# Seven counter increments ahead of the two loops of layer 1's experts

## The chip, the cores and the metric

The kernel runs on one core of one Trainium2 chip. The metric is the time of one execution on the device in microseconds. Before the change the median of 3 runs is 2973.64 us (2965.7 to 2974.67).

## What is computed

Two layers in float32 over 2048 token rows of width 512. Layer 0 is a state-space block over a context, then a mixture of experts; layer 1 is cross-attention, then a mixture of 32 experts with 8 chosen per token. Only that last mixture matters here:

```python
gate = jax.lax.ragged_dot(xs, w_gate, group_sizes)
up = jax.lax.ragged_dot(xs, w_up, group_sizes)
down = jax.lax.ragged_dot(jax.nn.silu(gate) * up, w_down, group_sizes)
routed = (down[unsort].reshape(T, K, H) * tkw[..., None]).sum(axis=1)
shared = jax.nn.silu(x @ sw_gate) * (x @ sw_up) @ sw_down
return (routed + shared).reshape(hidden_states.shape)
```

Every token row is copied once per expert that it goes to, the rows are grouped by expert, each group goes through gate, up and down of its expert, and the results are added back, scaled, to the token's row. An expert's weights are 512 x 256 for gate and up and 256 x 512 for down.

## The kernel before

`program` calls one function per stage: `mamba_stage`, `route_stage`, `expert_stage0`, `attention_stage`, `route_stage` again, and `expert_stage1`, which the change touches. Within a stage each engine has its own instruction stream, written out by hand in a function (`@block.vector`, `@block.scalar` and so on); semaphores set the order between them. There is no planner.

`expert_stage1` works on 144 tiles (`NTILE1`) of 128 rows; each half of 64 rows belongs to one expert. Per tile t the engines do this:

- SyncE loads weights of the next experts into a ring of four and announces them (`refill`, `announce`).
- ScalarE (`gate`, L1982 to L1984) computes the silu of the gate half of the product, issues loads of later rows (`reload`), scales and empties the output product (`empty`, L1991), and copies an expert's gate and up weights for the tile's second half (`copied`, L2006 to L2008).
- VectorE (`a_round`) turns the next tile's rows (`turned_rows`, L2082), copies the turned hidden rows `hT` of the tile before (L2087), makes the product `h` (L2092), works out scales and addresses (`addressed`, L2111 to L2118) and copies the down weights (`copied`, L2096 to L2100).
- TensorE turns the hidden rows of tile t - 1 (L2175), multiplies tile t by gate and up (L2166: 16 matmuls), then the hidden rows of t - 1 by down (L2188: 8 matmuls, which wait for `hT`).
- GpSimd adds the two halves' results to the output rows in device memory by two indirect DMAs (L1944), each waiting for an earlier one to land.

The rounds are of 16 tiles (`OUT`), 9 of them (`TURNS`). They are partly written out and partly loops in the program itself, with a compare and a branch at the end of the body. VectorE's round 0 is written out, rounds 1 to 7 are the loop `dve.Fori(1, TURNS - 1)` (L2148), and round 8 is written out. ScalarE's rounds 0 and 1 are written out, rounds 2 to 7 are the loop `act.Fori(2, TURNS - 1)` (L2057), and round 8 is written out. GpSimd loops over rounds 1 to 7 (L1971). TensorE has a loop of 4 tiles a turn.

`c["held"]` is a semaphore that engines count up and nobody reads. `hold` (L77) waits for a semaphore against a register's value and counts `held` up in the same instruction; `pause` (L980, a line of the route stage) counts it up alone, `dve.sem_inc(c["held"], 1)`.

Of the kernel before, what the change touches and what calls it, by code (L numbers as in the profile page):

```python
# [76 lines left out]
def hold(eng, sem, value, held):  # L77

    eng.wait_ge(sem, value)
    eng.sem_inc(held, 1)  # L80


class Pools:
# [1736 lines left out]
def expert_stage1(nc, c, I, D, x, route, W, out):  # L1820
# [3 lines left out]
    with ExitStack() as ctx:  # L1824
# [69 lines left out]
        def slots_written(eng, g):  # L1894
            count = eng.value_load(route["rows_held"][0:1, g:g + 1], min_val=16, max_val=16 * NT * K1 // LANES1)
            for lane in range(LANES1):
                hold(eng, written[lane], count, c["held"])

        with nc.Block(no_gpsimd_drain=True) as block:
# [80 lines left out]
            def _(act):  # L1980
                def gate(t, q):
                    act.wait_ge(sem["gu"], 1 + t + 1)  # L1982
                    act.wait_ge(sem["h"], 1 + t)
                    act.activation(sg[:, q % 2, :], ps_g[:, q % 2, 0:F1], ACT.Silu).then_inc(sem["sg"], 1)  # L1984

                def empty(t, q, first=False):
                    act.wait_ge(sem["down"], 1 + t + 1)
                    if not first:
                        act.wait_ge(sem["added"], 1 + t - OUT + 1)
                    act.wait_ge(sem["dest"], 1 + t + 1)  # L1990
                    act.activation(yo[:, q % OUT, :], ps_o[:, q % 2, :], ACT.Copy, scale=wrow[:, q % OUT, :])\  # L1991
                       .then_inc(sem["yo"], 1)
# [11 lines left out]
                def copied(t, q):  # L2004

                    e = act.value_load(ids[0:1, bass.ds(2 * t + 1, 1)], min_val=0, max_val=E - 1)  # L2006
                    hold(act, sem["ready"], 1 + e + 1, c["held"])
                    act.activation(cgu[:, q % 2, :, :], wgu[:, bass.ds(e % RING, 1), :, :].rearrange("p o k n -> p (o k) n"),  # L2008
                                   ACT.Copy).then_inc(sem["cgu"], 1)
# [5 lines left out]
                def reload(t, q):  # L2015
                    place, r = q % RING, q // RING % 2
                    known = isinstance(t, int)
                    group = t // RING if known else None
                    if place == RING - 2 and not (known and group + 2 >= GROUPS):
                        hold(act, sem["xsT"], 1 + t + 2, c["held"])  # L2020
                        if known:
                            rows_written(group + 2)
                        load_rows((t + RING + 2) * P, r, (0, 1))
                    if place == RING - 1 and not (known and group + 2 >= GROUPS):
                        load_rows((t + RING + 1) * P, r, (2,))
                    if place == 0 and not (known and group + 1 >= GROUPS):
                        load_rows((t + RING) * P, 1 - r, (3,))
                    if place == 1 and not (known and group + 1 >= GROUPS):
                        hold(act, sem["dest"], 1 + t - 1, c["held"])
                        load_rec((t + RING - 1) * P, 1 - r)  # L2030
# [21 lines left out]
                for q in range(1, OUT):  # L2052
                    gate(OUT + q, q)
                    reload(OUT + q, q)
                    empty(OUT + q - 1, q - 1)
                    copied(OUT + q + 2, q)
                with act.Fori(2, TURNS - 1) as i:  # L2057
                    for q in range(OUT):
                        gate(i * OUT + q, q)
                        reload(i * OUT + q, q)  # L2060
                        empty(i * OUT + q - 1, q + OUT - 1)
                        copied(i * OUT + q + 2, q)
# [10 lines left out]
            def _(dve):  # L2073
                def turned_rows(t, q, n, first=False):
                    if first:
                        dve.wait_ge(first_in, 16 * NQ)
                    elif q % RING == 0:
                        dve.wait_ge(rows_in[q // RING % 2], 16 * NQ * n)
                    if not first:
                        dve.wait_ge(sem["gu"], 1 + t - 1)  # L2080
                    part = slice(q % RING * NQ, (q % RING + 1) * NQ)
                    dve.transpose(xsT[:, q % 2, :, :].rearrange("p k (s j) -> p k s j", j=DQ),  # L2082
                                  xs[:, q // RING % 2, part, :].rearrange("p s (i k) -> p k s i", k=KH)).then_inc(sem["xsT"], 1)

                def turned_hidden(t, q):
                    dve.wait_ge(sem["htr"], 1 + t + 1)
                    dve.tensor_copy(hT[:, q % 2, :, :], ps_h[:, q % 2, 0:NW * P].rearrange("p (c s) -> p c s", s=P))\  # L2087
                       .then_inc(sem["hT"], 1)

                def product(t, q):  # L2090
                    dve.wait_ge(sem["sg"], 1 + t + 1)
                    dve.tensor_tensor(h[:, q % 2, :], ps_g[:, q % 2, F1:], sg[:, q % 2, :], ALU.mult).then_inc(sem["h"], 1)  # L2092

                def copied(t, q):

                    e = dve.value_load(ids[0:1, bass.ds(2 * t + 1, 1)], min_val=0, max_val=E - 1)  # L2096
                    hold(dve, sem["ready"], 1 + e + 1, c["held"])
                    if not (isinstance(t, int) and t < 2):
                        dve.wait_ge(sem["down"], 1 + t - 1)
                    dve.tensor_copy(cd[:, q % 2, :, :], wd[:, bass.ds(e % RING, 1), :, :].rearrange("p o k n -> p (o k) n"))\  # L2100
                       .then_inc(sem["cd"], 1)

                def addressed(t, q, n):
                    row = rec[:, q // RING % 2, q % RING, :]
                    word = token[:, q // RING % 2, q % RING * 2:q % RING * 2 + 2, 0]
                    if q % RING == 0:
                        dve.wait_ge(rec_in[q // RING % 2], 32 * n)
                    if not (isinstance(t, int) and t < OUT):
                        dve.wait_ge(sem["yo"], 1 + t - OUT + 1)
                        dve.wait_ge(sem["added"], 1 + t - OUT + 1)  # L2110
                    dve.scalar_tensor_tensor(out=mine[:, q % 2, :], in0=row[:, K1:2 * K1], scalar=slot1[:, bass.ds(t, 1)],  # L2111
                                             in1=row[:, 0:K1], op0=ALU.is_equal, op1=ALU.mult).then_inc(sem["named"], 1)
                    dve.scalar_tensor_tensor(out=pad[:, q % 2, :], in0=word, scalar=0.0,
                                             in1=spare1[0:HALF, q % 2 * 2:q % 2 * 2 + 2], op0=ALU.is_equal, op1=ALU.mult)\
                       .then_inc(sem["named"], 1)
                    dve.wait_ge(sem["named"], 1 + 2 * (t + 1))
                    dve.tensor_reduce(wrow[:, q, :], mine[:, q % 2, :], AX_X, ALU.add).then_inc(sem["chosen"], 1)
                    dve.scalar_tensor_tensor(out=dest[:, q, :], in0=pad[:, q % 2, :], scalar=-1.0, in1=word,  # L2118
                                             op0=ALU.add, op1=ALU.add).then_inc(sem["dest"], 1)

                def a_round(i, first=False, last=False):
                    for q in range(REST if last else OUT):
                        t = i * OUT + q
                        if first and q == 0:
                            dve.wait_ge(rows_in[0], 16 * NQ)
                        if not (last and q == REST - 1):
                            turned_rows(t + 1, q + 1, i * PER + (q + 1) // (2 * RING) + 1)
                        if not (first and q == 0):
                            turned_hidden(t - 1, q + OUT - 1)
                        product(t, q)  # L2130
                        addressed(t, q, i * PER + q // (2 * RING) + 1)
                        if not (last and q == REST - 1):
                            copied(t + 1, q + 1)
# [11 lines left out]
                turned_rows(0, 0, 1, first=True)  # L2145
                copied(0, 0)
                a_round(0, first=True)
                with dve.Fori(1, TURNS - 1) as i:  # L2148
                    a_round(i)
                a_round(TURNS - 1, last=True)  # L2150
# [1147 lines left out]
```

## Time and profile before

| | |
|---|---|
| median of 3 runs | 2973.64 us (2965.7 to 2974.67) |
| the profiled execution | 2954.43 us |
| its span | 2952.7 us |
| TensorE busy | 2631.0 us, 89% |
| VectorE busy | 1539.8 us, 52% |
| GpSimd busy | 1294.0 us, 44% |
| ScalarE busy | 1032.9 us, 35% |
| mean granted clock of TensorE | 0.962 |
| layer 1's experts | from about 2090 us to the end |

The profile is of one execution; all times below are from the start of its span. Busy is time in which an engine computes; register, branch and semaphore instructions and the issuing of DMAs are not counted. In a view of waits or a timeline, "[1.21 <-issue]" is idle time ahead of an instruction, with what ended it; "issue" means that it waited for nothing that the profile shows. The clock is in parts of full speed (1.00 is 2.4 GHz, 0.50 is 1.2 GHz); the mean of a stretch lies between.

### The profile page before, as it was taken

The page shows a single profiled execution, that of the slowest core. Times are in us where ns is not written, and L with a number is a line of the kernel's source. Part 1 is how long each engine was busy: PE and PEld are TensorE (multiplying, and loading weights), DVE is VectorE, ACT ScalarE, POOL GpSimd, SP SyncE. Part 2 cuts the span into 40 slices and gives each one's busy share as a digit, 9 for nine tenths or more (in the row PEclk, how much of TensorE's full clock was granted, in tenths as well). Part 3 has the DMA queues.
Part 4 walks back from the last instruction along what each step waited for, and adds up shares of the span by engine and source line. Part 5 has one row for each costly group of instructions (what it writes and reads, how often), then busy time and mean ns, then how long its engine had stood idle before and what let it go on. Part 6 is the DMA issues. An engine that isn't in the chain of part 4 may idle for free. (4 is left out here: it accounts for less than half of the span.)

```text
span 2952.7 us, 40958 instructions
## 1 busy us (share of the span) xinstructions
PE 2631.0 (89%) x11317; PEld 1089.2 (37%) x11318; DVE 1539.8 (52%) x2668; ACT 1032.9 (35%) x1305; POOL 1294.0 (44%) x935
## 2 busy tenths in 40 slices
PE   5889876699999987768999999799889999999998
PEld 2343432244444433323333333344333333333333
DVE  7999999741100033136666665551444544454554
ACT  4647464120000001023343433200344544455554
POOL 2767656312400023114564653145556656445454
PEclk8999999999999999889999999899999999999999
DMA  3333223301210269974047300154978877687764
GB/s 128 116 98 108 85 61 75 128 37 36 88 33 14 81 220 352 338 206 122 1 134 197 86 1 1 50 193 176 262 187 167 165 137 145 132 192 159 159 120 67
DMA packets 362080, 373.36 MB, mean 126 GB/s; under 512 B 85938, under 2 KB 268531, under 8 KB 361906
## 3 DMA queue, kind: packets, MB, share of 16 engines
q1 hardware_dynamic: 204098, 239.95, 26.1%
q0 software_dynamic: 45584, 93.26, 15.2%
q10 hardware_dynamic: 112224, 38.25, 6.3%
q8 instruction: 58, 0.95, 0.1%
q14 instruction: 116, 0.95, 0.1%
HBM read 231.96 MB, written 152.14 MB: 130 GB/s over the span
## 5 line engine op out<-in xcount | busy, mean ns | idle before, releaser
L1944 POOL DMA_INDIRECT out_x<-e_yo,e_dest x288 | 416.1, 1445 | 352.1 <-DMA out_x<-e_yo,e_dest 252.0
L2166 PE MATMUL e_psg<-e_wgu,e_xsT 128*64 x1152 | 522.0, 596 | 9.3 <-DVE e_xsT L2082 9.3
L2166 PE MATMUL e_psg<-e_cgu,e_xsT 128*64 128x512 f32 x1152 | 522.0, 596 | 0.0
L301 POOL TENSOR_TENSOR hc<-hs,bcst 128x1024 f32<-128x1024 f32 x128 | 300.6, 2349 | 178.9 <-DVE ps_b L521 171.7
L646 PE MATMUL ps_y<-hc,ident 128*128 128x512 f32 x512 | 240.9, 608 | 88.4 <-POOL hc L301 88.1
L2188 PE MATMUL e_pso<-e_wd,e_hT 128*64 x576 | 279.4, 608 | 33.0 <-DVE e_hT L2087 33.0
L527 DVE TENSOR_TENSOR_SCAN hs<-dA,ps_b 128x1024 f32<-128x1024 f32 x128 | 292.6, 2286 | 8.1 <-ACT dA L431 3.9
L2008 ACT ACTIVATE e_cgu<-e_wgu 128x2048 f32 x144 | 275.3, 1912 | 61.3 <-issue 33.9
L2188 PE MATMUL e_pso<-e_cd,e_hT 128*64 128x512 f32 x576 | 279.4, 608 | 0.0
L2166 PEld LDWEIGHTS e_psg<-e_wgu,e_xsT 128*64 128x64 f32 x1152 | 155.3, 138 | 259.0 <-issue 259.0
L949 ACT ACTIVATE r_sg<-r_ps_g 128x512 f32<-128x512 f32 x60 | 35.8, 597 | 525.0 <-PE r_ps_g L1258 525.0
L1277 PE MATMUL r_ps_t<-r_wd,r_h 128*128 128x512 f32 x480 | 210.9, 600 | 9.4 <-DVE r_h L1016 5.1
L1016 DVE TENSOR_TENSOR r_h<-r_ps_u,r_sg 128x512 f32<-128x512 f32 x60 | 41.4, 691 | 317.0 <-PE r_ps_u L1258 305.7
L431 ACT ACTIVATE dA<-dt,a_neg 128x511 f32<-128x511 f32 x256 | 165.3, 713 | 103.3 <-DVE hs L527 98.2
L717 POOL DMA_INDIRECT slots_in<-r_xn,scat x128 | 127.9, 999 | 165.8 <-DMA slots_in<-r_xn,scat 98.6
L2777 DVE TENSOR_REDUCE a_nm<-a_ps 128x2 f32<-128x992 f32 x128 | 146.1, 1185 | 88.4 <-PE a_ps L3021 88.0
L2539 ACT ACTIVATE a_pt<-a_ps 128x1024 f32<-128x1024 f32 (+1 forms) x128 | 126.2, 1022 | 181.4 <-PE a_ps L3038 120.6
L2092 DVE TENSOR_TENSOR e_h<-e_psg,e_sg 128x256 f32<-128x256 f32 x144 | 61.1, 425 | 233.7 <-ACT e_sg L1984 233.6
L2082 DVE STREAM_TRANSPOSE e_xsT<-e_xs 128x512 f32<-128x512 f32 x144 | 171.1, 1188 | 19.7 <-issue 8.6
L1991 ACT ACTIVATE e_yo<-e_pso,e_wrow 128x512 f32<-128x512 f32 x144 | 99.1, 688 | 234.4 <-PE e_pso L2188 215.9
L646 PEld LDWEIGHTS ps_y<-hc,ident 128*128 128x128 f32 x512 | 92.7, 191 | 231.2 <-POOL hc L301 137.0
L2100 DVE COPY e_cd<-e_wd 128x1024 f32 x144 | 101.3, 703 | 142.1 <-PE e_pso L2188 136.7
(432 smaller groups left out, 4205.7 us busy)
## 6 DMA issues: line engine op xcount, KB each, us to landing
slots_in<-zeros SPq DMA_DIRECT2D x144, 256.0 KB
e_xs<-slots_in ACTq DMA_DIRECT2D x140, 256.0 KB
bcst<-bc_rows SPq DMA_DIRECT2D x128, 256.0 KB, 4.2
e_wgu<-in_wg SPq DMA_DIRECT2D x32, 512.0 KB, 5.2
e_wgu<-in_wu SPq DMA_DIRECT2D x32, 512.0 KB, 6.5
e_wd<-in_wd SPq DMA_DIRECT2D x32, 512.0 KB, 8.3
e_w<-in_wg SPq DMA_DIRECT2D x11, 1408.0 KB, 15.9
e_w<-in_wu SPq DMA_DIRECT2D x11, 1408.0 KB, 17.6
```

Source lines behind the costliest of these rows:

```text
L301: pool.tensor_tensor(hc[:, it % 2, half(h), :], hs[:, it % 2, half(h), :], bc(bcst[:, q, 1, :], 1, HB), ALU.mult).then_inc(sem["hc"], 1)
L431: i = act.activation(dA[:, it % 2, t, 1:], dt[:, b % 2, t, 1:], ACT.Exp, scale=a_neg[:, n, t:t + 1])
L527: dve.tensor_tensor_scan(hs[:, it % 2, half(h), :].rearrange(flat), dA[:, it % 2, half(h), :].rearrange(flat), ps_b[:, :, :].rearrange(fla ...
L646: i = pe.matmul(ps_y[:, t, :], c["ident"][:, :], hc[:, it % 2, t, :], start=False, stop=False, skip_group_check=True)
L717: pool.indirect_dma_start(D["xs1"][:, :], bass.IndirectOffsetOnAxis(route["scat"][:, t, k:k + 1], 0), route["xn"][:, t, 0:H + 2 * K1 + 1], ...
L1277: i = pe.matmul(ps_t[:, j % 2, :], h[:, f, j * P:(j + 1) * P], wd[:, f, :], start=f == 0, stop=f == FC - 1)
L1944: pool.indirect_dma_start(out[:, :], bass.IndirectOffsetOnAxis(dest[:, q, s:s + 1], 0), yo[half(s), q, :], None, bounds_check=T + 2 * P - ...
L2008: act.activation(cgu[:, q % 2, :, :], wgu[:, bass.ds(e % RING, 1), :, :].rearrange("p o k n -> p (o k) n"), ACT.Copy).then_inc(sem["cgu"], 1)
L2082: dve.transpose(xsT[:, q % 2, :, :].rearrange("p k (s j) -> p k s j", j=DQ), xs[:, q // RING % 2, part, :].rearrange("p s (i k) -> p k s i ...
L2166: j = pe.matmul(ps_g[half(s), q % 2, :], xsT[:, q % 2, k, half(s)], w, start=k == 0, stop=k == KH - 1, tile_position=(0, s * HALF), skip_g ...
L2188: j = pe.matmul(ps_o[half(s), q % 2, :], hT[:, q % 2, a, half(s)], w, start=a == 0, stop=a == NW - 1, tile_position=(0, s * HALF), skip_gr ...
L2777: dve.tensor_reduce(nm[:, i % 8, 2 * z:2 * z + 2], ps[:, at:at + 2, 0:S2], AX_X, ALU.max, negate=True)\
```

## The change

A helper that counts the semaphore up n times, called once by ScalarE with 4 and once by VectorE with 3, each just ahead of that engine's loop. Nothing else is changed, and nothing reads the counter. The instructions behind the two places stand four and three instructions later in their engines' programs.

```diff
+def placed(eng, n, held):
+
+    for _ in range(n):
+        eng.sem_inc(held, 1)
...
                     empty(OUT + q - 1, q - 1)
                     copied(OUT + q + 2, q)
+                placed(act, 4, c["held"])
                 with act.Fori(2, TURNS - 1) as i:
                     for q in range(OUT):
                         gate(i * OUT + q, q)
...
                 copied(0, 0)
                 a_round(0, first=True)
+                placed(dve, 3, c["held"])
                 with dve.Fori(1, TURNS - 1) as i:
                     a_round(i)
```

## Rows read from the trace of the kernel before

**Rows 1.** The page, busy us, share of the span and instructions.

```profile
PE 2631.0 (89%) x11317; PEld 1089.2 (37%) x11318; DVE 1539.8 (52%) x2668; ACT 1032.9 (35%) x1305; POOL 1294.0 (44%) x935
```

**Rows 2.** Windows: busy us of PE, PEld, DVE, ACT, POOL; clock, DMA share, GB/s.

```profile
2095.00:2183.00 88.00, 88.00 (x506) 34.02 (x504) 46.53 (x124) 46.90 (x47) 41.97 (x41) 1.00 0.94 273
...
2376.00:2393.00 17.00, 13.80 (x62) 4.95 (x60) 5.96 (x16) 5.45 (x6) 10.27 (x7) 0.80 0.58 86
...
2762.00:2773.00 11.00, 8.40 (x54) 3.44 (x52) 5.33 (x15) 3.58 (x5) 4.78 (x4) 1.00 0.43 65
...
2855.00:2938.00 83.00, 83.00 (x480) 33.10 (x478) 43.47 (x119) 42.57 (x44) 42.07 (x30) 1.00 0.52 78
```

**Rows 3.** Waits of TensorE from 2210 us on: total us, times, longest.

```profile
PE e_pso L2188 <- DVE e_hT L2087: 23.4, 7, 7.0
```

**Rows 4.** Timeline of VectorE, two tiles: start, us, line, operation, idle before.

```profile
2397.20 0.42 DVE L2092 TENSOR_TENSOR e_h<-e_psg,e_sg 128x256 f32<-128x256 f32 x1 [1.76 <-ACT e_sg L1984]
2397.54 0.22 DVE L2111 SCALAR_TENSOR_TENSOR e_mine<-e_rec,e_slot 128x8 f32<-128x8 f32 x1
...
2469.83 0.42 DVE L2092 TENSOR_TENSOR e_h<-e_psg,e_sg 128x256 f32<-128x256 f32 x1 [1.77 <-ACT e_sg L1984]
```

**Rows 5.** The loops' own instructions, by line: ns, first and last start us.

```profile
L2148 DVEq COMPARE_BRANCH  x7: 55/62/77, 2279.9 to 2851.6; - x7
...
L1971 POOLq COMPARE_BRANCH  x7: 44/53/53, 2338.8 to 2862.2; - x7
```

**Rows 6.** Chain of waits across VectorE's second branch: start us, us, what.

```profile
2376.08 0.07 DVEq L2148
2376.16 3.32 issue
...
2380.66 1.21 issue
...
2382.50 3.68 PE e_pso L2188 x8
...
2391.15 1.72 PE e_pso L2188 x8
```

**Rows 7.** Timeline of ScalarE behind its first taken branch.

```profile
2382.11 0.39 ACT L1984 ACTIVATE e_sg<-e_psg 128x256 f32<-128x256 f32 x1 [3.80 <-issue]
```

**Rows 8.** Timeline of GpSimd across its last branch.

```profile
2862.39 1.41 POOL L1944 DMA_INDIRECT out_x<-e_yo,e_dest  x1 [0.56 <-issue]
```

**Rows 9.** DMA, the instruction queue: from 2376.3 to 2471: packets, MB, share.

```profile
q14 instruction: 10, 0.08, 0.3%
```

**Rows 10.** Timeline of VectorE at its 128th to 132nd instruction of a turn.

```profile
2515.13 0.42 DVE L2092 TENSOR_TENSOR e_h<-e_psg,e_sg 128x256 f32<-128x256 f32 x1 [1.64 <-ACT e_sg L1984]
2515.76 0.25 DVE L2111 SCALAR_TENSOR_TENSOR e_mine<-e_rec,e_slot 128x8 f32<-128x8 f32 x1 [0.21 <-issue]
```

**Rows 11.** The single increments of the counter on VectorE, ns min/median/max.

```profile
L982 DVEq EVENT_SEMAPHORE  x16: 21/21/21, 624.1 to 1981.2; - x16
```

**Rows 12.** Timeline of VectorE in the first tile of its loop.

```profile
2193.96 0.23 DVE L2111 SCALAR_TENSOR_TENSOR e_mine<-e_rec,e_slot 128x8 f32<-128x8 f32 x1 [10.52 <-POOLq L1960]
```

**Rows 13.** Timelines of a plain tile, VectorE and then TensorE.

```profile
2372.03 0.47 DVE L2087 COPY e_hT<-e_psh 128x256 f32<-128x256 f32 x1
...
2373.55 0.59 PE L2188 MATMUL e_pso<-e_wd,e_hT 128*64 x1
```

**Rows 14.** Timeline of TensorE behind VectorE's second branch.

```profile
2382.50 1.11 PE L2188 MATMUL e_pso<-e_wd,e_hT 128*64 x1 [3.20 <-DVE e_hT L2087]
```

**Rows 15.** Chain of waits across VectorE's sixth branch.

```profile
2759.27 2.80 issue
...
2765.08 1.94 PE e_pso L2188 x8
```

**Rows 16.** Timeline of GpSimd, first scatters of tiles 16 and 64.

```profile
2261.61 1.41 POOL L1944 DMA_INDIRECT out_x<-e_yo,e_dest  x1 [0.41 <-DMA out_x<-e_yo,e_dest]
...
2495.82 1.41 POOL L1944 DMA_INDIRECT out_x<-e_yo,e_dest  x1 [2.13 <-ACT e_yo L1991]
```

## The prediction
> **What bounds the kernel now.** I read the page's busy times first: TensorE is busy for 2631.0 of 2952.7 us and every other engine for about half of the span or less [rows 1]. So an edit is worth what it does to the idle time and the clock of TensorE. Layer 1's experts are the last 860 us. The view by windows splits them: the first 88 us (the first 16 tiles, written out) and the last 83 us are full, 88.00 of 88.00 and 83.00 of 83.00 us at clock 1.00, but around each turn of the loops there is a hole: 13.80 of 17.00 us busy at clock 0.80, and late in the stage 8.40 of 11.00 at clock 1.00 [rows 2]. The waits of TensorE name one releaser in this stage, VectorE's copy of `hT`: 23.4 us in 7 waits, the longest 7.0 [rows 3].
>
> The period shows what such a hole costs in full. Undisturbed, a tile takes 5.587 us: `h` of two tiles 13 apart starts at 2397.20 and 2469.83 [rows 4]. VectorE's loop turns 7 times, the branches lying between 2279.9 and 2851.6 us [rows 5]. That is six turns of 16 tiles, 571.7 us, where 96 undisturbed tiles are 96 x 5.587 = 536.4. So the six turns carry 35.3 us that are not tiles, 5.9 each. After the seventh branch, which falls through, TensorE runs on without a gap, as do the 16 tiles of the first round [rows 2].
>
> **What the 35.3 us are.** The chain of waits shows the second taken branch: the branch at 2376.08, then 3.32 us of "issue", in which VectorE waits for nothing that the profile shows, then the transpose, then another 1.21 us of "issue" before the copy of `hT`, and only then TensorE's down product; its 8 matmuls take 3.68 us where the next tile's take 1.72, because the clock has fallen to 1.2 GHz in the pause [rows 6]. ScalarE has the same hole 0.4 us later: 3.80 us before its `sg`, no releaser [rows 7]. GpSimd turns a loop over the same 16 tiles, with its branches up to 2862.2, and has its scatters 0.56 us apart at the last of them [rows 5, 8]. So a taken branch as such costs well under a microsecond, and VectorE and ScalarE lose theirs to something else.
>
> I take it to be code loading. In the turn from 2376.3 to 2471 the instruction queue q14 moves 10 packets of 0.08 MB in all, 8 KB each [rows 9]. Laid over the recorded instructions, they come in pairs, one for VectorE and one for ScalarE: at the branch, after VectorE's second and ScalarE's first instruction, a few instructions on, and then some way after the 130th and the 260th. The places where an engine steps over a block edge can be seen too: VectorE's step from its 130th to its 131st instruction of a turn, between `h` and `mine`, takes 0.63 us from start to start (2515.13 to 2515.76), and 0.34 elsewhere (2397.20 to 2397.54) [rows 4, 10]. ScalarE has such steps after its 1st, 129th and 257th. So a block is 128 instructions; VectorE's loop begins two instructions ahead of a block edge and ScalarE's one ahead. Counted in the trace, a turn is 330 instructions on VectorE, 301 on ScalarE, 378 on GpSimd. GpSimd's marks lie at its 256th instruction of a turn, so its loop begins at about slot 1 of a block and 378 instructions lie in exactly three blocks, and it reloads nothing. VectorE's and ScalarE's 330 and 301 fit three blocks as well, but lie across four: 2 + 128 + 128 + 72 and 1 + 128 + 128 + 44. An engine that holds four blocks and always loads the next one in order has then dropped the block of the loop's head by the time it branches.
>
> **The change, part by part.** (a) Three increments on VectorE. Increments of this counter on VectorE stand elsewhere in the kernel as single instructions: 16 of them, 21 ns each [rows 11]. I take one instruction each, 3 x 21 = 63 ns, once, at the loop's entry. In its first tile VectorE stands 10.52 us at its first `mine` of that round, waiting for GpSimd's scatters [rows 12]; they are hidden in that, and would cost 0.06 us otherwise. (b) Four on ScalarE, once: 84 ns by the same row. TensorE waits for nothing of ScalarE's from 2210 us on [rows 3], and `h`, the step of VectorE behind `sg`, is not what it waits for either. Hidden. Nobody reads the counter, and no transfer is passed.
>
> (c) Where the loops come to lie. VectorE's head moves from slot 126 to 129, which is slot 1 of the next block: 1 + 330 = 331 of 384 slots, three blocks. ScalarE's moves from 127 to 131, slot 3: 3 + 301 = 304 of 384, three blocks. With the block prefetched behind them that is four, GpSimd's case. Neither then loads at its branch. What remains of a taken branch is GpSimd's: its scatters keep 0.56 us from end to start across it [rows 8]. VectorE has cover for that: in a plain tile `hT` ends at 2372.50 and the down product starts at 2373.55, 1.05 us later [rows 13]. So I count nothing. Block edges inside the body move by three or four instructions; VectorE's come to lie ahead of `h`, which waits 1.6 to 1.8 us for ScalarE anyway [rows 4, 10]; their 0.3 us are hidden there.
>
> Bounds of (c). The most is the whole excess, 35.3 us. The least, if both engines still missed at the branch but no longer just behind it: `hT` comes 1.2 us earlier per turn, TensorE's pause of 3.20 us [rows 14] falls to about 2.0, 6 x 1.2 = 7 us, and the clock's part stays. Below nothing would need a fifth load per turn, and 10 packets are what two engines with four blocks and one ahead already need. I take 35.3, since the row nearest to the new position is GpSimd's, and it is clean.
>
> **What the Trainium skill says.** GpSimd's branches cost nothing over three blocks [rows 5, 8]. The Trainium skill (Runtime: NRT & Kernel Launch, "Instruction fetch mechanics") has the code memory as two blocks of 256 instructions, and a taken branch out of them as a stall for a load. The packets of 8 KB [rows 9] speak for smaller blocks than that. Taken with small blocks, its two lines would leave every branch of VectorE and ScalarE a miss after the change too; that is rival A, which gains 7 to 20 us. By its 256-instruction blocks the sum would be the full one, as a body of 330 just behind an edge lies in two.
>
> **The sum.** The profiled execution took 2954.43 us (span 2952.7 and 1.7 around it). Less 35.3 plus 0 is 2919.1. The runs' median, 2973.64, is 19.2 above the profiled execution; I leave that distance as it is, as nothing in it belongs to the branches: 2973.6 - 35.3 = 2938.3. What is late next after the repair is TensorE itself, at 5.587 us per tile.
>
> **Rivals.**
> A. The branches still miss, and only the load just behind them goes. For: two of the five loads per turn are serial now, 3.32 and 1.21 us [rows 6], and a position change surely mends the second. Against: GpSimd. Gain: 6 x 1.2 = 7 us, and up to 13 more where the shorter pause keeps the clock, as the late turns did (2.80 us at the branch and the 8 matmuls in 1.94 [rows 15]): 2954 to 2967, middle 2960.
> B. It does not do what it says: like increments are folded into one, or whoever places the loops moves their heads back. VectorE would come to slot 127, where the same two loads stay. For: nothing in the trace shows three in a row on one counter. Against: the 16 single ones. Time: 2973.6.
> C. Slower: GpSimd's scatters. They hold VectorE once, 10.52 us at tile 16 [rows 12]. The pauses of TensorE give them time to catch up. Tile 16's first scatter is at 2261.61 and tile 64's at 2495.82 [rows 16]: 78.1 us for 16 tiles against the 89.4 that TensorE would take. It decides from the point where 16 tiles of scatters take longer than the 95.3 us of a turn now. At 100 us, eight rounds from 2183 on are 800 us, not the 756 of now: 3018 us. Against: 78.1.
> D. Only one of the two engines is mended, or another stall stays under the clock: VectorE alone decides the first taken branch (ScalarE still runs written-out code there), so half the gain or more: about 2952.
>
> **Chances.** Forecast 0.78, A 0.09, B 0.06, C 0.02, D 0.05. Its own spread is some 8 us, since one turn (at 2567) was 3.6 us dearer than its like and the runs themselves lie 9 us apart. The range is 2926 to 2954, which takes in D and the near end of A. A difference of 0.3%, 9 us, is about what can be told from nothing here. Faster by more: forecast, D and four fifths of A, 0.90; within: B and the rest, 0.07; slower: C and a remainder, 0.03.
>
> **What would show it.** Right: the "issue" holes behind the branches of VectorE and ScalarE gone; four branch spacings of about 89.4 us; TensorE's clock 1.00 in all loop turns; few packets on q14 in a turn, 0 or near it where 10 were; waits for `hT` near zero. Rival A: branch holes of about 3 us with the 1.21 gone, 6 to 10 packets. B: everything as before. C: VectorE's `mine` waiting for GpSimd in later rounds. Wrong would be, above all, a loop head that is not where I count it: a body still over four blocks.

## The result, and the profile after

The changed kernel takes 2923.5 us (median of 4 runs, 2922.83 to 2931.45), the kernel before 2969.67 (4 runs, 2964.71 to 2974.67) beside it. The ratio is 0.9852, 95% interval [0.9827, 0.9877]: faster, by 44 us by the ratio and 46.2 by the medians, where 35.3 were forecast. The time is 2.5 us below the range.

Three later comparisons, with 20, 18 and 15 runs of before, gave 0.9898 [0.9869, 0.9927], 0.9891 [0.9868, 0.9914] and 0.9897 [0.9861, 0.9933]. By these ratios the change is worth 30 to 32 us, and the medians differ by 34.9, 35.4 and 32.6. So the saving is 30 to 35 us, and the first comparison stands out.

The page of the profiled execution after (its own time 2931.45 us): its span, the engines' busy times, TensorE's granted clock by slices, and the instruction queue, which had 116 packets before.

```profile
span 2929.8 us, 40965 instructions
...
PE 2626.8 (90%) x11317; PEld 1088.7 (37%) x11318; DVE 1540.4 (53%) x2668; ACT 1032.7 (35%) x1305; POOL 1295.3 (44%) x935
...
PEclk8999999999999999888999999999999999999999
...
q14 instruction: 61, 0.50, 0.1%
```

The program has 7 instructions more (40965 against 40958). The view by line shows them, each its own instruction, 21 ns on VectorE and 17 on ScalarE:

```profile
L86 ACTq EVENT_SEMAPHORE  x4: 17/17/17, 2292.5 to 2293.1; - x4
L86 DVEq EVENT_SEMAPHORE  x3: 21/21/21, 2193.5 to 2193.6; - x3
```

VectorE's loop branches, by line; they answer to [rows 5]. From first to seventh it is 536.6 us where it was 571.7, and 96 undisturbed tiles are 536.4:

```profile
L2156 DVEq COMPARE_BRANCH  x7: 50/56/77, 2292.2 to 2828.8; - x7
```

The chain of waits over VectorE's second branch (2381.6 us), which answers to [rows 6]. Neither hole is left: the chain stays on TensorE, whose 8 down matmuls take 1.72 us as in any tile.

```profile
2379.32 1.72 PE e_pso L2196 x8
2381.03 0.44 PE e_psh L2183 x8
2381.47 3.43 PE e_psg L2174 x16
2384.90 1.72 PE e_pso L2196 x8
```

VectorE's timeline there: after the copy of the down weights, which is the last work of a turn, the transpose and the copy of `hT` follow at once.

```profile
2381.59 0.69 DVE L2107 COPY e_cd<-e_wd 128x1024 f32 x1 [0.94 <-PE e_pso L2196]
2382.20 1.14 DVE L2089 STREAM_TRANSPOSE e_xsT<-e_xs 128x512 f32<-128x512 f32 x1
2383.26 0.39 DVE L2094 COPY e_hT<-e_psh 128x256 f32<-128x256 f32 x1
2385.45 0.42 DVE L2099 TENSOR_TENSOR e_h<-e_psg,e_sg 128x256 f32<-128x256 f32 x1 [1.80 <-ACT e_sg L1990]
2385.84 0.23 DVE L2118 SCALAR_TENSOR_TENSOR e_mine<-e_rec,e_slot 128x8 f32<-128x8 f32 x1
```

ScalarE's `sg` behind the branch, which stood 3.80 us without a releaser [rows 7], now waits 1.13 us for TensorE:

```profile
2385.03 0.38 ACT L1990 ACTIVATE e_sg<-e_psg 128x256 f32<-128x256 f32 x1 [1.13 <-PE e_psg L2174]
```

The DMA queues from 2381.6 to 2471 us, a turn of the loops, as in [rows 9]. The instruction queue (q14) is not in the list: no packet, where it had ten.

```profile
q0 software_dynamic: 2970, 4.86, 39.4%
q10 hardware_dynamic: 12820, 4.43, 24.5%
q1 hardware_dynamic: 2400, 3.15, 11.0%
```

The windows, as in [rows 2]: VectorE's second branch is in the first, the loops from 2206 us on in the second, those from VectorE's first branch on in the third, and the written-out end in the fourth. The 3.2 us without work in the second lie ahead of the first branch.

```profile
2376.00:2393.00 17.00, 17.00 (x100) 6.58 (x98) 8.99 (x25) 9.19 (x10) 10.64 (x8) 1.00 0.71 111
2206.00:2822.00 616.00, 612.77 (x3496) 237.14 (x3498) 327.70 (x880) 325.20 (x327) 355.99 (x245) 0.99 0.79 161
2293.00:2822.00 529.00, 529.00 (x3028) 204.47 (x3026) 282.38 (x759) 282.23 (x284) 305.47 (x211) 1.00 0.79 163
2822.00:2905.00 83.00, 83.00 (x478) 32.13 (x476) 43.33 (x117) 44.76 (x45) 43.57 (x32) 1.00 0.56 87
```

TensorE's waits for `hT` from 2210 us on, which answer to [rows 3] and were to come near zero:

```profile
PE e_pso L2196 <- DVE e_hT L2094: 7.8, 2, 7.1
```

The 7.1 us ended at 2209.2 and are not of a branch. VectorE's wait for GpSimd's scatters at tile 16 [rows 12] ended at 2205.4 in this execution, 11.5 us later than in the one before, and so falls into the stretch. The other wait, 0.7 us, is at the last tile. None is left at a branch.

### The profile page after: what moved, and what is told of

Same layout as the page of the kernel before. It is cut to its first block and busy times, and to the rows that moved or that the text cites. A ratio compares the mean times of both kernels' runs of the same rounds, so it can differ in the third digit from the quotient of the medians.

```text
span 2929.8 us, 40965 instructions
## 1 busy us (share of the span) xinstructions
PE 2626.8 (90%) x11317; PEld 1088.7 (37%) x11318; DVE 1540.4 (53%) x2668; ACT 1032.7 (35%) x1305; POOL 1295.3 (44%) x935
## 5 line engine op out<-in xcount | busy, mean ns | idle before, releaser
L2196 PE MATMUL e_pso<-e_wd,e_hT 128*64 x576 | 272.6, 596 | 9.7 <-DVE e_hT L2094 8.8
L2196 PE MATMUL e_pso<-e_cd,e_hT 128*64 128x512 f32 x576 | 272.6, 596 | 0.0
```

What stands on the lines that cost most here:

```text
L2196: j = pe.matmul(ps_o[half(s), q % 2, :], hT[:, q % 2, a, half(s)], w, start=a == 0, stop=a == NW - 1, tile_position=(0, s * HALF), skip_gr ...
```

## Experiments

**Each engine alone.** First VectorE's three increments without ScalarE's four.

```diff
-                placed(act, 4, c["held"])
```

> VectorE's three increments alone; ScalarE's loop stays one instruction ahead of a block edge. Theory (a body across four blocks reloads at the branch, a body in three does not): VectorE's five loads of a turn are gone and ScalarE's five stay, so 5 packets a turn on q14, and the first taken branch, where only VectorE branches, is clean. ScalarE's hole of about 3 us at the branch and 2.3 us behind it stays and holds its silu, so about as much as before is lost at the other five: 2960 us at most, 2950 if half of it is covered. Rival (VectorE alone decides, since TensorE waits for its hT): the whole gain, 2924 us.

Measured 2940.12 us, ratio 0.9944 [0.9926, 0.9961]. Half of the gain. The waits of TensorE show a new releaser, `h`, which is late because ScalarE's `sg` is, five times, once per taken branch of ScalarE:

```profile
PE e_psh L2183 <- DVE e_h L2099: 12.1, 5, 5.7
```

Between the first and the seventh branch lie 551.2 us, an excess of 14.8 (excess is what a kernel takes there beyond the 536.4 us of 96 undisturbed tiles). So ScalarE's reloads cost some 3 us of TensorE's time each where VectorE's are gone, and the time is 10 us below the least that I expected.

The packets are best counted over the whole execution, from the pages, since a window of 93 us can reach into the next turn (it showed 6 here). They are 61 in after, 86 here, 91 in a4_only below and 116 in before: five for each of ScalarE's five taken branches, and five for each of VectorE's six. The lines of the pages of v3_only, a4_only and before:

```profile
q14 instruction: 86, 0.70, 0.1%
q14 instruction: 91, 0.75, 0.1%
q14 instruction: 116, 0.95, 0.1%
```

Then ScalarE's four without VectorE's three:

```diff
-                placed(dve, 3, c["held"])
```

> ScalarE's four increments alone; VectorE's loop stays two instructions ahead of a block edge. Theory: VectorE's hT is what TensorE waits for, 5 packets a turn are left, and nearly the whole loss stays: 2960 to 2970 us. Rival (the two engines' losses add up): half the gain, about 2947 us.

Measured 2958.81 us, ratio 0.9999 [0.9988, 1.0011]: nothing. The branches span 569.4 us, an excess of 33.0, and TensorE waits for `hT` as before:

```profile
PE e_pso L2196 <- DVE e_hT L2094: 24.7, 6, 7.7
```

The losses don't add up. The two engines miss at the same time, VectorE's hole covers ScalarE's, and only mending both gives the whole.

**Is it the count of blocks, or the place right behind an edge?** After, with 56 increments on VectorE, then with 57:

```diff
-                placed(dve, 3, c["held"])
+                placed(dve, 56, c["held"])
```

> After, but VectorE counts up 56 times: its head comes to slot 54 of a block, and 54 + 330 = 384 slots are three blocks to the last slot. Theory (what counts is the number of blocks that the body touches): as after, 2924 us, no packet of the instruction queue in a turn. Rival (being right behind a block edge is what helps, or the loader moves such a head): packets and stalls come back, 2940 us or more.

Measured 2922.84 us, 0.988 [0.9861, 0.9899]; no packet in a turn; the branches 536.3 us apart in all. As after, with the head at slot 54 of a block.

```diff
-                placed(dve, 56, c["held"])
+                placed(dve, 57, c["held"])
```

> One increment more than v56_fits: the head at slot 55, the last instruction of the body in a fourth block. Theory: VectorE loads again, about five packets a turn, and its branch waits about 3 us; but 73 instructions lie behind the head in its block, so the second stall (1.2 us before hT) does not come back. hT is then 1.9 us late for TensorE in six turns: 11 us and up to 20 with the clock, so 2935 to 2955 us. Rival (distance to the edge behind the head is what costs): as v56_fits, 2924 us.

Measured 2949.92 us, 0.9973 [0.9959, 0.9986]. One instruction more costs 27 us. The branches by line, and under them the instruction queue in one turn:

```profile
L2156 DVEq COMPARE_BRANCH  x7: 55/63/77, 2285.0 to 2843.8; - x7
```

```profile
q14 instruction: 5, 0.04, 0.2%
```

558.8 us from first to seventh is an excess of 22.4. The chain of waits across the second branch shows one hole and not two: 3.69 us behind the branch, nothing of note ahead of `hT`.

```profile
2379.09 0.07 DVEq L2156
2379.16 3.69 issue
2382.85 0.06 DVEq L2156
...
2383.63 0.34 issue
2383.97 0.39 DVE e_hT L2094
2384.36 0.19 issue
2384.55 1.94 PE e_pso L2196 x8
```

This decides for the count of blocks: 54 + 330 = 384 = 3 x 128 fits and 385 does not. It also fixes the edge to the instruction. a4_only has the same miss and the load right behind the head as well. Its excess is 33.0, so the second load's share is 10.6 us in six turns; by the two medians it is 8.9, so 1.5 to 1.8 us a turn. That is rough, since the excess of one and the same kernel varies by 6 us from profile to profile, as the repeats below show.

**Both engines over, heads far from the edge.** VectorE 57 increments, ScalarE 85:

```diff
-                placed(act, 4, c["held"])
+                placed(act, 85, c["held"])
```

> Both engines' bodies across four blocks again, but with heads far ahead of the block edge: VectorE's at slot 55, ScalarE's at slot 84 (84 + 301 = 385). About 10 packets of the instruction queue a turn, as before. Theory (the miss at the branch costs about 3 us, the load just behind a head that has one or two instructions left costs the rest): faster than before by what the second load costs, 1.2 us and what of the clock goes with it in six turns, 7 to 15 us; about as v57_over. Rival (only the number of packets counts): as before. Rival (distance behind the head is all): as after.

Measured 2950.19 us, 0.998 [0.996, 1.0], one of its ten runs far out at 8263 us. Ten packets in a turn, 561.4 us between the branches, an excess of 25.0, where before has 29 to 35. The packets are as many as before and the median is 7.6 us less than that of before beside it, at the edge of the noise. It is also as slow as v57_over, which loads half as many packets. So the number of packets is not the cost; that they come in a row behind the branch is part of it. This is the state of rival A of the prediction, made by hand.

**The edge, by one instruction.** After, with VectorE's increments set to 1 and to 2:

```diff
-                placed(dve, 3, c["held"])
+                placed(dve, 1, c["held"])
```

> VectorE counts up once, ScalarE four times: VectorE's head goes from slot 126 to 127, its body still touches four blocks, and one instruction is left behind the head instead of two. Theory: five packets a turn, both loads in a row, with the transpose now behind the second of them: as a4_only or 1 us a turn slower, 2957 to 2965 us. Rival (the places are counted wrong by one or two, or increments fold): as after, 2923 us.

Measured 2967.45 us, 1.003 [1.0019, 1.004], slower than before and the slowest of all: the branches span 578.7 us, an excess of 42.3. The transpose, which TensorE's next tile and `hT` wait behind, now lies behind the second load too: at the second branch VectorE stands 2.86 us, does one instruction, and stands again until 5.59. The price was 2.5 us beyond what I had given.

```diff
-                placed(dve, 1, c["held"])
+                placed(dve, 2, c["held"])
```

> VectorE counts up twice: its head at slot 0 of a block, the body over three blocks from the first slot on. Theory: as after, 2923 us, and no packets in a turn. Rival (the head is one slot further back than counted, at 127): four blocks, as v1_edge.

Measured 2923.95 us, 0.9884 [0.9865, 0.9903], no packet in a turn, 536.4 us between the branches. One instruction, 43 us. The head is where it was counted, and every increment is one slot.

**The third engine.** By its count GpSimd's body of 378 fits only from slots 0 to 6, and it begins at 1. After, with six increments ahead of its loop:

```diff
+                placed(pool, 6, c["held"])
                 with pool.Fori(1, TURNS - 1) as i:
```

> After, with six increments ahead of GpSimd's loop too: its body of 378 goes from slot 1 to slot 7, 7 + 378 = 385 slots, one more than three blocks hold. Theory: five packets a turn on the instruction queue come back, GpSimd stands about 3 us at each branch, and the time is that of after within 3 us, since its scatters have 20 us and more in hand. Rival (its head is not where I counted it, or its memory is larger): no packets. Rival (scatters are near the bound): 10 us or more slower than after.

Measured 2935.82 us, 0.9924 [0.99, 0.9948]: 13 us more than after, where I had expected 3 at most. The reload came as foreseen (91 packets on the page against 61, five for each of GpSimd's six taken branches), and TensorE does not notice it (536.3 us between VectorE's branches). But from GpSimd's branch to the second instruction behind it 3.7 to 7.0 us pass, where 0.24 to 0.28 do in after. Six increments were tried and not five, so that the edge lies exactly at slot 384 here too is not shown. The scatters no longer catch up by the end. GpSimd's last scatter in this kernel, and then in the one after:

```profile
2930.71 1.41 POOL L1950 DMA_INDIRECT out_x<-e_yo,e_dest  x1 [0.30 <-issue]
```

```profile
2925.03 1.41 POOL L1950 DMA_INDIRECT out_x<-e_yo,e_dest  x1 [0.31 <-DMA out_x<-e_yo,e_dest]
```

ScalarE hands over the last tile at 2918.0 us there and at 2921.1 in after, so the scatters end 14.1 us behind it instead of the 5.3 of every other kernel here. What I took for slack toward VectorE was none toward the end of the kernel.

**Why some reloads are dearer.** VectorE's fourth branch costs more than the others in every kernel where VectorE reloads: 4.30 us to the next instruction in before, where the other five take 2.86 to 3.41. The traces show what is different there. Behind the third and the fourth branch of before (windows of 5 us, the last number is the DMA traffic in GB/s), and then behind GpSimd's fifth in pool_over:

```profile
2471.70:2476.70 5.00, 3.25 (x16) 0.86 (x12) 1.66 (x2) 2.03 (x2) 1.41 (x1) 1.00 0.31 52
2567.30:2572.30 5.00, 3.23 (x16) 0.85 (x12) 1.19 (x2) 2.00 (x2) 3.84 (x3) 1.00 0.78 224
```

```profile
2700.40:2705.40 5.00, 5.00 (x32) 2.00 (x30) 2.89 (x8) 2.85 (x3) 1.26 (x1) 1.00 1.11 303
```

SyncE issues the three loads of an expert's weights at the time of that fourth branch, the first of them here:

```profile
2566.93 0.56 SPq L1814 DMA_DIRECT2D e_wgu<-in_wg  x1
```

At the fourth branch the traffic is 224 GB/s in before, 240 in v57_over (5.48 us) and 268 in v1_edge (4.46 us); at the other branches of these kernels it is 120 or less. In pool_over GpSimd's steps take 6.1 to 6.9 us where it is 263 to 303, and 3.6 to 4.7 where it is 97 to 151. So a reload seems to come later when the weights are being moved beside it. That is read off the traces and was not tested by moving the loads, and it isn't the whole: one step of ScalarE in before_fourth took 5.22 us at 86 GB/s.

**Where the other 10 us came from.** Both kernels again, unchanged, three times, the second and the third time on one chip, since the mechanism was then settled and the size was not.

```diff
 (no edit)
```

> The kernel before, unchanged, for a second profile and a second set of times. Open is why the first comparison gave 46 us where the profile had 35. U1 (the reloads at the branches cost more in most executions than in the one profiled): a profile whose time is above 2960 shows more than 40 us between the first and the seventh branch beyond 96 tiles, and the first h of the stage near 2094 us. U2 (the stages ahead differ from one execution to the next, and the change has no part in it): the excess stays at 33 to 37 us and the first h moves by the difference.

2956.4 us, ratio 0.9998 [0.9983, 1.0013]; its profiled execution took 2956.47. Excess 29.2 us (565.6 between the branches), the first branch at 2288.2.

> The changed kernel, unchanged, beside before on the same chip. Theory with U2: 34 to 36 us less than before on average. U1: 40 or more less where before is slow. Profile: six turns of 89.4 us in either case, and the first h of the stage somewhere between 2094 and 2105 us.

2922.84 us (2920.85 to 2929.31), profiled 2920.85; 536.4 us between the branches, the first at 2281.6.

> The kernel before once more. So far 43 runs of it lie at 2956 to 2958 us in the median, the four beside which the change was first timed at 2965 to 2975, while the changed kernel has 2923 in both. V1 (the reloads are dearer in some executions or on some chips): a profile at 2965 us or more would show 40 us and more between the first and the seventh branch beyond 96 tiles, and one at 2957 about 29 to 35. V2 (something ahead of the loops): the excess is 29 to 35 us whatever the time, and the first branch comes later instead.

2954.15 us, 0.9988 [0.9975, 1.0], profiled 2956.24. Excess 34.2 (570.6), the first branch at 2282.8.

> The changed kernel beside it: 2923 us if the 12 us belong to the reloads (V1), whatever before has; above 2930 where before is above 2965 if they belong to the stages ahead (V2).

2923.19 us (2920.35 to 2929.56).

> The kernel before on another occasion. V1 (the reloads are dearer in some executions): a profile at 2965 us or more shows 40 us and more of excess between the first and seventh branch. V2 (the stages ahead or the wait for the scatters at tile 16): 29 to 36 us of excess and a later first branch. If all its runs are near 2957 again, the 12 us stay open.

This time before was high and wide: 2964.1 us over 10 runs, and 2965.91 (2951.18 to 2977.16) over the 15 beside it. Its profiled execution took 2964.32, with an excess of 35.5 (571.9) and the first branch at 2289.3.

> The changed kernel beside it: 2923 us by V1 whatever before has, 2930 and more where before is above 2965 by V2; 34 us below before if before is at 2957.

2933.35 us (2926.92 to 2940.12): the changed kernel was 10 us up as well. Its branches, and then those of after_third:

```profile
L2156 DVEq COMPARE_BRANCH  x7: 50/56/77, 2288.9 to 2825.2; - x7
```

```profile
L2156 DVEq COMPARE_BRANCH  x7: 50/56/77, 2281.8 to 2818.2; - x7
```

The spans are 2926.4 and 2919.3. All 7.1 us of the difference lie ahead of the first branch; the six turns (536.3 and 536.4) and the stretch behind them (101.2 and 101.1) are equal. The excess of before does not grow with its time either: 29.2, 34.2 and 35.5 us at 2956.5, 2956.2 and 2964.3, and 35.3 at 2954.4. So V2: executions differ ahead of the first branch, in both kernels, and the change does not touch that.

Only part of the 7.1 us lies in the stages ahead, though. The first `h` of the stage starts at 2098.3 us in after_fourth and at 2095.9 in after_third, 2.4 later; the other 4.7 us arise in the stage's first 32 tiles. TensorE has a hole there, in after_fourth and then in after_third:

```profile
2150.00:2170.00 20.00, 13.58 (x62) 4.62 (x58) 3.92 (x13) 3.06 (x4) 13.73 (x14) 0.83 0.68 214
```

```profile
2150.00:2170.00 20.00, 20.00 (x120) 7.83 (x118) 10.07 (x30) 9.95 (x11) 9.87 (x11) 1.00 0.92 270
```

before_fourth has the same hole (14.38 of 20 us busy). Some of it comes back, as VectorE's wait for the scatters at tile 16, 9.9 us in after_third, is missing in both profiles of the fourth occasion.

## Why the prediction was right in kind and missed in size

- *The hole and its price (35.3 us in six turns).* Right. The branches after lie 536.6 us apart, 35.1 less. The later pairs differ by 34.9, 35.4 and 32.6 us in their medians and by 30 to 32 by their ratios. The excess of before was 29.2 to 35.5 in four profiles, so the one that I had read was at the upper end.
- *Code loading, blocks of 128, four blocks against three.* Right, and now shown: fit and no fit differ by one instruction at both ends of the body, slots 127 and 0 at the head, 384 and 385 at the tail, for VectorE. For ScalarE (127 against 131) and GpSimd (1 against 7) the loads come and go with the count, but their edges are not fixed to the instruction. The packets follow, 10, 5 or none in a turn. The bound that speaks of "a fifth load" is miscounted: five loads a turn were there already.
- *"A taken branch as such costs well under a microsecond."* Right, but the row that it rests on [rows 8] is of GpSimd's seventh branch, which falls through. Its six taken branches in before show it: 0.24 to 0.37 us from the branch to the second instruction behind it.
- *(a) and (b), the increments cost nothing; one slot each.* Right, and ScalarE's took 17 ns each and not 21; rival B falls.
- *(c) Nothing is left of a taken branch.* Right to 0.2 us in all six.
- *Rival A.* Its state was built in both_over: 25.0 us of excess are left, so it would have gained 4 to 10 us, about the lower end of the 7 to 20 that I gave. It is not this kernel's case. The Trainium skill (Runtime: NRT & Kernel Launch, "Instruction fetch mechanics") would have a memory of two blocks of 256 instructions. By that, v1_edge and v2_on_edge, whose heads are at 127 and at the next 0, could differ by their 43 us only if the edge between them were one of a 256-block. Then v56_fits and v57_over, which end at 384 and 385 counted from that edge, would both fit into the 512 slots behind it; they differ by 27 us. The two pairs together, and the packets of 8 KB, decide against it.
- *Rival C.* It did not happen, but it was nearer than priced: pool_over lost 13 us at the end of the kernel. In the prediction I looked at the scatters' lead over VectorE only.
- *Rival D.* Half right: VectorE alone gains half (v3_only), 16 us, where I had priced it at 21.6.
- **The step that failed: "The runs' median, 2973.64, is 19.2 above the profiled execution; I leave that distance as it is, as nothing in it belongs to the branches."** That nothing in it belongs to the branches holds; that it stays does not. The same distance, from the profiled execution to the median of the runs beside it, was 8.0 us the other way in the changed kernel (2931.45 against 2923.5), where the sum had put it at 19.2. In the later pairs it was 0.1, 2.1 and 0.2 us the other way for before, and 2.0, 2.2 and 5.3 for after. So the 19.2 belonged to those three runs: on the three occasions before the fourth, 77 runs of before took 2948.34 to 2967.02. The saving itself was sized right. Counted from the profiled execution, 2954.43 - 35.3 = 2919.1 us is 4.4 from what was measured; counted from the high median it was 14.8 off, and the range began at 2926, above the first of the two. That 2919.1 comes so close is in part luck, as a profiled execution can itself be 8 us off.
- *What stays open.* Three of the four times of before in the first comparison had been taken earlier than the changed kernel's. That an occasion can be 10 us up is shown in the fourth pair, for both kernels; that it was so for those three runs alone is an inference. What makes the hole in the stage's first tiles, and the rest of what differs ahead of the first branch, stays open too.

No kernel here beats the changed one; v56_fits, v2_on_edge and the repeats are its equals.

## What to carry to other kernels

A loop in the program whose body just fits the blocks that an engine keeps (here three of 128 instructions) is fast or slow by where it begins: here one instruction ahead of it was worth 43 us in 2950. If a profile shows idle time with no releaser just behind a loop's branch, count the body's instructions, look whether the instruction queue moves packets in every turn, and move the head; do it for each engine that loops, as one mended engine alone gained half and the other nothing. And take the base for a forecast from many runs. Where three runs stand 19 us away from the profiled execution, count from both and let the range hold both results.

## What the runs showed of the hardware

- VectorE, ScalarE and GpSimd load code in packets of 8 KB. For VectorE one covers 128 instructions (edges at 127 against 0 and at 384 against 385); for the other two the counts agree with that. A loop body over three such blocks turns without a load; one that reaches into a fourth costs five packets at every taken branch (pages of 61, 86, 91 and 116 packets).
- A miss at a taken branch is a hole of 2.8 to 4.3 us on VectorE, and of 4.3 to 5.5 at its fourth branch, where the DMA traffic is 224 to 268 GB/s and not 120 or less. The tile there took 11.87 us in before and 12.85, 12.02 and 12.36 in its repeats; at the others it took 7.9 to 9.2, and once 10.7.
- A block edge just behind the head costs a second load in a row, 1.2 us ahead of `hT` [rows 6] and 1.5 to 1.8 us a turn in the sum.
- After a pause of 3.20 us [rows 14] TensorE's granted clock was 0.50, its lower level (3.68 us for eight matmuls instead of 1.72 [rows 6]). After one of 2.60 us at the sixth branch it was 1.00 (1.94 us for the eight [rows 15]).
- Two engines that miss side by side don't add up: VectorE's repair alone was worth 16 us, ScalarE's alone nothing, both together 30 to 35.
